# A language-model layer on one core: last head normalised from the sums in its output bank, output weights split ahead of the router's, router masks and slot tables on GpSimd

## The reference, cut to what matters

```python
# attention, 16 heads, three branches with their own softmax
out = g[0] * attn(q, k1, v1, causal) + g[1] * attn(q, ks, vs) + g[2] * attn(q, kw, vw, causal)
h = x + out.reshape(T, 16 * 32) @ w_proj
# layer norm, router over 8 experts, top 2 with jitter-masked softmax weights
m1 = max(scores); mask1 = (m1 - scores) / max(abs(scores), m1) > 2 * 0.01
w1 = softmax(where(mask1, -inf, scores))[argmax(scores)]
# the same again with the first choice struck out: m2, mask2, w2
y = h + sum over the two choices of w * w_down(silu(w_gate x) * (w_up x))
```

## Time and profile before

| what | us |
|---|---|
| median of 3 runs | 2762.03 (2761.5 to 2763.81) |
| the profiled execution | 2753.63 |
| its span, first to last instruction | 2751.9 |
| embedding to first head | 0 to some 400 |
| last head, first unit to last matmul | some 2221 to 2324.8 |
| mix, first load to last DVE step | 2343.8 to 2463.7 |
| first gather of the experts | 2464.85 |

### The profile page before, as it was taken

The page is one execution under the profiler, slowest core; times in us unless marked ns, Lnnn a source line. Parts: engine busy times, 40 slices in busy tenths (PEclk is TensorE's granted clock), DMA queues, the critical chain, the costliest instruction groups (busy, mean ns, idle before and its releaser), DMA issues. The chain is left out here.

```text
span 2751.9 us, 38402 instructions
## 1 busy us (share of the span) xinstructions
PE 2330.5 (85%) x12402; PEld 1854.9 (67%) x12402; DVE 1771.9 (64%) x2824; ACT 1751.0 (64%) x3574; POOL 1629.8 (59%) x1430
## 2 busy tenths in 40 slices
PE   0278569999989999999899999989999997448885
PEld 0155347777767777777777777767777776438885
DVE  2566357677666868676775868666676863455553
ACT  3433227777767777777677777768778786116663
POOL 5055326767566766757576776856656565006885
PEclk9975569999999999999999999999999999659998
DMA  9757553415051533415151533222132110615776
GB/s 384 320 191 244 173 131 104 115 44 139 20 154 28 142 64 103 127 32 143 32 139 29 147 67 96 65 62 61 28 72 49 32 25 17 186 69 176 193 206 169
DMA packets 199860, 314.87 MB, mean 114 GB/s; under 512 B 95915, under 2 KB 130219, under 8 KB 186731
## 3 DMA queue, kind: packets, MB, share of 16 engines
q1 hardware_dynamic: 189947, 298.23, 37.8%
q0 software_dynamic: 9712, 14.18, 2.7%
HBM read 210.20 MB, written 101.75 MB: 113 GB/s over the span
## 5 line engine op out<-in xcount | busy, mean ns | idle before, releaser
L1390 POOL TENSOR_TENSOR p_lo<-prob,p_hi 128x512 fp32r<-128x512 f32 (+2 forms) x960 | 1091.5, 1146 | 636.5 <-ACT p_hi L1468 465.0
L1466 ACT ACTIVATE prob<-ps_s 128x512 f32<-128x512 f32 (+4 forms) x1344 | 725.2, 540 | 477.2 <-PE ps_s L1483 387.7
L1601 DVE TENSOR_REDUCE max_part<-ps_x 128x1 f32<-128x128 f32 (+1 forms) x1240 | 719.4, 607 | 220.7 <-PE ps_x L1512 128.4
L1468 ACT ACTIVATE p_hi<-ps_s 128x512 fp32r<-128x512 f32 (+3 forms) x1344 | 718.8, 535 | 1.6
L1390 DVE TENSOR_TENSOR p_lo<-prob,p_hi 128x512 fp32r<-128x512 f32 (+1 forms) x320 | 267.5, 836 | 145.2 <-ACT p_hi L1468 134.7
L1569 PE MATMUL ps_o<-p_hi,v_win 128*128 128x512 f32 (+3 forms) x640 | 253.2, 396 | 0.0
L1569 PE MATMUL ps_o<-p_hi,v_lat 128*128 128x512 f32 (+3 forms) x640 | 246.6, 385 | 0.0
L1571 PE MATMUL ps_o<-p_lo,v_win 128*128 128x512 f32 (+3 forms) x640 | 236.4, 369 | 0.0
L1571 PE MATMUL ps_o<-p_lo,v_lat 128*128 128x512 f32 (+3 forms) x640 | 234.3, 366 | 0.0
L1662 DVE TENSOR_TENSOR raw_o<-ps_o,low_sum 32x512 f32<-32x512 f32 x192 | 131.3, 684 | 74.1 <-ACT low_sum L1454 58.7
L1512 PE MATMUL ps_x<-k_hi,q_hi 96*128 96x512 f32 (+2 forms) x320 | 121.6, 380 | 39.4 <-DVE max_part L1601 39.3
(11 more groups left out here) (432 smaller groups left out, 5846.7 us busy)
## 6 DMA issues: line engine op xcount, KB each, us to landing
raw<-in_experts_w_dram SPq DMA_DIRECT2D x23, 1536.0 KB, 7.3
wbuf<-in_tok_weight_dram SPq DMA_DIRECT2D x16, 2000.0 KB, 16.9
head_first<-kw_scratch SPq DMA_DIRECT2D x72, 256.0 KB, 5.0
kw_scratch<-st_hi SPq DMA_DIRECT2D x48, 256.0 KB, 2.4
kw_scratch<-st_lo SPq DMA_DIRECT2D x48, 256.0 KB, 3.1
q_scratch<-st_hi SPq DMA_DIRECT2D x48, 256.0 KB, 3.7
q_scratch<-st_lo SPq DMA_DIRECT2D x48, 256.0 KB, 5.2
head_first<-q_scratch SPq DMA_DIRECT2D x48, 256.0 KB, 6.3
```

The lines of the kernel that those rows point to most:

```text
L1390: ns.tensor_tensor(upper if low else p_lo[:, i % LSLOTS, c:CH], prob[low:P, i % NPROB, c:CH], upper.bitcast(F32), ALU.subtract).then_inc(s ...
L1466: nc.scalar.activation(prob[low:P, i % NPROB, c:CH], ps_s[i % 3][low:P, c:CH], ACT.Exp, scale=SCALE).then_inc(s["p_full"], 1)
L1468: nc.scalar.activation(p_hi[:, i % SLOTS, c:CH], ps_s[i % 3][:, c:CH], ACT.Exp, scale=SCALE).then_inc(s["p_up"], 1)
L1601: ins = nc.vector.tensor_reduce(mpart[:, q, c:c + 1], bank[:, 0:w], axis=AX.X, op=ALU.max)
```

## The change

In the last head DVE takes, for each output, the reciprocal of rows 0 to 31 of the bank into `turned` (unused there by then), then the add as before, then one scalar_tensor_tensor that multiplies by the gate and the reciprocal. Window and select are summed at unit 56, latent after the last output. The stores and loads of the last head's sums and weights go, and ACT's first latent copy waits for the select outputs to be read instead.

In mix ACT splits `wp` without waiting for `rw`; `rw` is split after the second chunk. DVE waits for h only at the first residual. The router's lower part is made after the first four residuals, and PE waits for it before the first logits.

In the router DVE keeps maximum and choice. The test (m - s) / max(|s|, m) > 0.02 becomes two tests with a subtraction, on POOL, with the sizes 0.02 |s| from DVE; POOL also strikes out the first choice and multiplies by the exponential. DVE sums and takes reciprocals after the running count. POOL makes the token product of `r_vals` and the last quarter of `ohb`, as eight tensor_scalar.

```diff
@@ attend: low_stored
-            if b == LATENT or h:
+            if b == LATENT and h == H - 1:
+                eng.wait_ge(s["o_read"], read_count(SELECT, NJ - 1, h))
+            elif b == LATENT or h:
@@ attend: SP, end of each head, and after the last
                 store_rows(h, 0)
-                store_sums(h, 2)
                 if nxt:
+                    store_sums(h, 2)
                     load_kw(h + 1, 1)
                     load_v(h + 1, WINDOW)
-                store_sums(h, 0)
-                if nxt:
+                    store_sums(h, 0)
                     store_rows(h + 1, 1)
-            store_sums(H - 1, 1)
-            load_sums(H - 1)
-            store_inverse(H - 1)
-            load_weight(H - 1)
             store_output(H - 1)
@@ attend: dve_output
+            own = slice(j * DV, (j + 1) * DV)
+            o = raw_o[own, h % 2, br, :]
+            if h == H - 1:
+                nc.vector.reciprocal(turned[own, br, :], ps_o[BANK[out]][0:DV, :])
+            nc.vector.tensor_tensor(o, ps_o[BANK[out]][DV:2 * DV, :],
                                     low_sum[64 * (j % 2):64 * (j % 2) + DV, low_slot(b), j // 2, :], ALU.add).then_inc(s["o_read"], 1)
+            if h == H - 1:
+                dve.wait_ge(s["o_read"], read_count(b, j, h))
+                nc.vector.scalar_tensor_tensor(o, o, gates[own, br, 0:1], turned[own, br, :], ALU.mult, ALU.mult).then_inc(s["norm1"], 1)
+        def last_sum(dve, br):
+            first = raw_o[:, (H - 1) % 2, 0, :]
+            if br == 2:
+                dve.wait_ge(s["norm1"], 8)
+            else:
+                dve.wait_ge(s["norm1"], 12)
+                dve.wait_ge(s["done"], 2 * H - 1)
+            nc.vector.tensor_tensor(first, first, raw_o[:, (H - 1) % 2, br, :], ALU.add).then_inc(s["done"], 1)
@@ attend: DVE
+                if h == H - 1:
+                    dve.wait_ge(s["back"], 2 * len(PREP) // 3)
...
+                    if h == H - 1 and i == HU + 12:
+                        last_sum(dve, 2)
...
-            for step in range(6):
-                dve_finish(dve, H - 1, step)
+            last_sum(dve, 1)
@@ mix: POOL, after its constants
+            for n in range(2):
+                m, keep = top["m%d" % (n + 1)], sc["keep%d" % n]
+                pool.wait_ge(s["m"], n + 1)
+                f.add(nc.gpsimd.tensor_tensor(sc["dist"][:], wide(m[:]), logit[:], ALU.subtract))
+                f.add(nc.gpsimd.tensor_scalar(top["t2"][:], m[:], 2.0 * JITTER, None, ALU.mult))
+                f.wait()
+                f.add(nc.gpsimd.tensor_tensor(keep[:], sc["dist"][:], wide(top["t2"][:]), ALU.subtract))
+                if n == 0:
+                    pool.wait_ge(s["size"], 1)
+                f.add(nc.gpsimd.tensor_tensor(sc["far"][:], sc["dist"][:], sc["size"][:], ALU.subtract))
+                f.wait()
+                f.add(nc.gpsimd.tensor_scalar(keep[:], keep[:], 0.0, None, ALU.is_gt))
+                f.add(nc.gpsimd.tensor_scalar(sc["far"][:], sc["far"][:], 0.0, None, ALU.is_gt))
...
+                pool.sem_inc(s["ex"], 1)
+                f.add(nc.gpsimd.tensor_tensor(keep[:], keep[:], sc["far"][:], ALU.mult))
+                f.wait()
+                f.add(nc.gpsimd.tensor_scalar(keep[:], keep[:], -1.0, 1.0, ALU.mult, ALU.add))
...
+                pool.wait_ge(s["exd"], n + 1)
+                nc.gpsimd.tensor_tensor(keep[:], keep[:], sc["ex"][:], ALU.mult).then_inc(s["kept"], 1)
+            pool.wait_ge(s["col"], 1)
+            for c in range(2):
+                n = slice(c * NT, (c + 1) * NT)
+                nc.gpsimd.tensor_tensor(vals[:, n, 0, :], oha[:, n, :], tokid[:].unsqueeze(2).to_broadcast([P, NT, NCOL]), ALU.mult).then_inc(s["tok"], 1)
+            for n in range(24, N2):
+                nc.gpsimd.tensor_scalar(ohb[:, n, :], iota_b[:], sb[:, n:n + 1], None, ALU.is_equal).then_inc(s["ohb3"], 1)
@@ mix: PE
-            pe.wait_ge(s["whi"], 2)
-            pe.wait_ge(s["wlo"], 2)
+            pe.wait_ge(s["wlo"], 1)
...
+                if j == 0:
+                    pe.wait_ge(s["wlo"], 2)
...
+            pe.wait_ge(s["tok"], 2)
@@ mix: ACT
             act.wait_ge(s["w"], 16)
-            act.wait_ge(s["rw"], 32)
             nc.scalar.copy(wp_hi[:], wp[:]).then_inc(s["whi"], 1)
-            nc.scalar.copy(rw_hi[:], rw[:]).then_inc(s["whi"], 1)
...
+            upper_outputs(0)
+            upper_outputs(1)
+            act.wait_ge(s["rw"], 32)
+            nc.scalar.copy(rw_hi[:], rw[:]).then_inc(s["whi"], 1)
+            upper_outputs(2)
@@ mix: DVE, sizes and gate
+            nc.vector.tensor_scalar(sc["size"][:], logit[:], -2.0 * JITTER, None, ALU.mult).then_inc(s["minus"], 1)
+            dve.wait_ge(s["minus"], 1)
+            nc.vector.scalar_tensor_tensor(sc["size"][:], logit[:], 2.0 * JITTER, sc["size"][:], ALU.mult, ALU.max).then_inc(s["size"], 1)
...
+            def weigh(n):
+                dve.wait_ge(s["kept"], n + 1)
+                step(nc.vector.tensor_reduce(top["sum"][:], sc["keep%d" % n][:], axis=AX.X, op=ALU.add))
+                step(nc.vector.reciprocal(w12[:, n, :], top["sum"][:]))
@@ mix: DVE, tables
-            for c in range(2):
-                n = slice(c * NT, (c + 1) * NT)
-                v.add(nc.vector.tensor_tensor(vals[:, n, 0, :], oha[:, n, :], cols(tokid[:], NT), ALU.mult))
...
-            for q in range(4):
+            for q in range(3):
```

## The result

The change made the kernel slower: 2793.72 us median of 4 runs (2787.63 to 2801.67) against 2762.92 us for the kernel before on the same chip, a ratio of 1.0118 (95% interval 1.0097 to 1.0139), or +30.8 us by the medians (+32.6 by the ratio). I had forecast 2773.5 and a range up to 2787: the sign was right, the size of +11.5 was not.

A forecast was written before the change was run, and what follows sets the result against it. TensorE was taken to set the last head's pace, with 14.6 us of VectorE time to spare; +18.5 - 10.2 + 2.4 - 1.0 + 1.8 = +11.5 us gave a median of 2773.5, range 2759 to 2787 (8 in 10).

The forecast's parts named there:

- Last head, first eight outputs: Window and select outputs: VectorE's 33.1 us of added work exceeds 14.6 us idle, so TensorE stalls by +18.5 us.
- a bound of 28: High end of the last head's +18.5 us: each stall is 3.5 us because idle time comes in the wrong place.
- Latent half: Last head's latent outputs: 25 us idle against three outputs, costed at nothing, with 1 us possible.
- Tail: Last head's serial end up to the output's store: 15.8 us becomes 5.6 us, -10.2 us.
- Output weights: Mix block: no gain, as the second chunk lands no sooner; TensorE idles and its clock falls, +2.4 us.
- Masks: Router: masks move to GpSimd, which becomes the bound; gain of 1.8 us less collisions with VectorE, -1.0 us.
- Tables: Slot tables: GpSimd's and VectorE's products exclude each other, TensorE starts later, last quarter in time, +1.8 us.
- Rival C: Last head: TensorE's clock falls in six stalls of about 3 us, 9 us more, 2782.5 us; chance 0.14.
- A: Last head: reciprocal takes 0.69 us instead of 3.35, the tail is pure gain, -8.4 us, 2753.6; chance 0.10.
- B: Last head: VectorE's extra work is mostly swallowed, stall 12 us, total -2.6 to +4, around 2763 us; chance 0.16.
- D: Mix: output weights were the lock, TensorE and all behind it start 6.5 us earlier, +2.6, 2764.6 us; chance 0.03.

The follow-up runs named there:

- x8: x1 with no reciprocal, each last-head output only multiplied by its gate (division left out); 2763.86 against 2771.05 us before, ratio 0.9958.
- x4: x1 with a copy of the same tile in place of VectorE's reciprocal (division left out); 2771.26 us, ratio 1.0028 to the kernel before.
- x9: x1 with ten filler score products on TensorE at each of six stall places; 2797.92 against 2764.35 us before, ratio 1.0114.
- x6: x1 with the addition first and each reciprocal in four pieces of 128 columns behind the next units' steps; 2790.98 against 2771.05 us before, ratio 1.0067.
- x7: Kernel before, with only latent outputs normalised from their sums, in pieces; window and select still through memory, during the latent half; 2765.67 against 2771.05 us, ratio 0.9976.
- x10: x7 with three large steps set further apart and the change's router masks on GpSimd; 2758.05 against 2764.35 us before, ratio 0.9966.
- x1: Only the attention part of the change, on the kernel before; 2796.26 against 2765.99 us, ratio 1.0106.
- x12: x10 with the latent outputs' reciprocals whole instead of in four pieces; 2759.14 against 2762.57 us before, ratio 0.9985.
- x2: Only the output-weights order of the change, on the kernel before; 2766.62 us, ratio 0.9998.

## Why the prediction was wrong, by its steps

- **Last head, first eight outputs: +18.5 forecast, +34.4 measured (+32.4 with the attention part alone).** The durations and the count were right: VectorE's work grew by 27.6 us over the seven gaps, and 7 x 4.14 is 29. What failed is the sentence "they add 8 x 4.14 = 33.1 us where 14.6 are free". At this dose none of it was free (at that of x8, 2 us of 5.1 were). VectorE's idle time before, 11.1 us in this part, consists mainly of waits in a ring: 4.5 us for ACT's copy of the very output (5.5 with the wait just before the first), and 3.4 us for maxima that TensorE makes only into banks that VectorE frees. A step in the ring moves the next wait with it. x4 shows it without any long instruction, x9 at a granted clock of 0.97. The sentence itself had a bound of 28, "because idle time comes in the wrong place"; that was the mechanism, and even it left a fifth out.
- **Latent half: nothing forecast, +6.9 measured.** "Idle is ample" was true (28.9 us) and no argument. A whole reciprocal delays VectorE's share of the lower halves, and TensorE's value products wait for these, 4.1 us in three waits where there was none. With pieces the half is 2.0 (x6), 2.1 (x7) and 1.6 us (x10) longer than before, with whole reciprocals 6.6 (x1) and 5.8 (x12).
- **Tail: -10.2 forecast and measured.** A serial chain with nothing beside it is the one place where a sum of durations is the answer.
- **Output weights: +2.4 forecast, nothing measurable.** No gain, since the second chunk is late: right. The loss at the low clock: wrong in its cause, since nine of the twelve profiles without the edit have it too. I had compared two chunks of one profile and taken the fast one for the rule.
- **Masks: -1.0 forecast, -0.75 measured.** GpSimd is the bound, as said; VectorE waits 4.96 us for its last mask. GpSimd's comparisons took 0.53 us each, where I had 0.25.
- **Tables: +1.8 forecast, +1.84 measured, and the agreement is luck.** I had TensorE start 1.8 us late and the last quarter in time. It starts 0.75 us late (7.07 us after the slots' last step instead of 6.32), and the rest is the last quarter, which is not in time. The exclusion itself is in the trace. In the tables the two engines take turns: GpSimd's two products end 1.28 us after VectorE's product beside each has ended, and VectorE's second product (2.91 us and not 1.68) and first quarter (2.32 and not 1.22) end 1.6 and 1.1 us after GpSimd's. So it cost VectorE 2.3 us, two thirds of the 3.5 that I charged: what was over is the price of GpSimd's product. The Trainium skill, "SBUF — State Buffer", Who interferes with whom, has a VectorE instruction with two inputs in SBUF and a GpSimd one that reads SBUF exclude each other; the trace agrees.
- **Rival C** was half right: the clock does fall in the stalls (0.79 over 89 us). The Trainium skill, "TensorE: Matmul & The Clock Gate", Part 1, has the clock fall after an idle spell; the trace agrees. I priced it at 9 us beyond the stall (and a low spell at 2.2 us, where the ratio of the earlier trace rows gives 5.2 x (1 - 3.73 / 6.13) = 2.0). x9 gives at least 2.7 us in five gaps, an estimated 4 over the stretch if the other gaps are like them. **A** falls with the 3.35 us, **B** and **D** with x4 and x2.

Put together afterwards with what the runs showed, the sum is +27.7 of VectorE's work in the first part taken one for one, some 4 for the clock, 7 for the latent half, -10.2 and +1.1: +29.6, against +30.8 by the medians. The 4 is that estimate, and no run shows it for the whole stretch.

## What to carry to other kernels

Before you let added work vanish in an engine's idle time, ask what each idle spell waits for: if it waits for an engine that in turn waits for this one, it is poor cover. Here an added microsecond cost 0.6 at the smallest dose, 0.8 in pieces and some 1.2 otherwise. Where the work has to stand in such a ring, cut it into pieces and spread them (in the first part 32.3 us of work in pieces cost 26.2, 28.3 us of whole reciprocals and products 35.7), and move what can be moved to a stretch in which the engine isn't in the ring's way. In this kernel that turned +1.1% into -0.3% (x1, x10); most of it is the move, since x10 with whole reciprocals (x12) is at -0.15% already (0.03% of either is the masks). And compare profiles by stretches between events: that of the last head repeats to 0.02 us where its code is the same, while whole executions of the same kernel differ by 20. Not every stretch is so steady: that from the output weights' issue to the logits, with its loads, varies by 4 us.

## What was unexpected in the hardware

- VectorE's reciprocal takes 0.17 us at 4 elements, 0.35 at 32, 0.45 at 48, 0.94 at 128, 1.75 at 256 and 3.35 at 512. All six lie within 0.01 us of 0.145 us and 6.25 ns for each element (right behind another piece one of 128 shows 0.88). The tile of 512 is copied in 0.68 us.
- GpSimd's tensor_scalar with one scalar for each partition took 0.60 us for a piece of 128x128 alone, and 2.63 and 1.31 beside VectorE's products. Its tensor_tensor of 128x736 with a broadcast operand took 2.86 us beside VectorE's products; what it takes alone no run shows.
- A VectorE product with two tensor inputs in SBUF that starts beside a GpSimd subtraction ends 0.54 to 0.55 us after it: so four of the twelve in the changed kernel took 1.26 to 1.69 us and not 0.74. The product of x8, with one tensor input, stood beside GpSimd nine times of twelve and took 0.47 to 0.49 us each time.
- Six stalls of TensorE of 3.15 to 3.7 us came with a granted clock of 0.79 over 89 us, where it was 1.00 before: it spent two fifths of them at the lower of its two levels (1.2 GHz), although it had work again after each stall. Shorter ones came with a low clock too: in x4 the stalls are of 1.1 to 2.1 us, and the granted clock of the first part is 0.88.
